# Perceiver block on one core: statistics before normalising, GpSimd normalises half of the tiles, first masks, keys and values between the query projections

## The chip, the cores and the metric

The kernel runs on one core of a Trainium2 chip, as one program. The metric is the device time of one execution in microseconds (us), median over several. Five engines work side by side and meet at semaphores: TensorE (PE; its weight loads are PEld), VectorE (DVE), ScalarE (ACT), GpSimd (POOL) and SyncE (SP), which here only issues DMAs. L12 is line 12 of the kernel before.

## The reference, cut to what matters

Three blocks follow each other on x (128 batches of 32 queries, width 128); each normalises its input. The change lies in front of, and at the start of, the first.

```python
x = x + xattn(layernorm(x), ctx_1024, ctx_1024, mask, Wq, bq, Wk, bk, Wv, bv, Wo, bo)
x = x + attn(layernorm(x), w_q, w_k, w_v, w_o)      # rotary, 16 query heads, 4 key heads
x = x + ffn(layernorm(x), Wg, W1, W2)               # 8 experts, one for each token
# xattn, 16 heads of width 8, 257 keys to a batch:
Q, K, V = heads(query @ Wq + bq), heads(key @ Wk + bk), heads(value @ Wv + bv)
energy = where(mask == 0, -1e9, Q K^T / sqrt(8)); out = softmax(energy) V; return out @ Wo + bo
```

## The kernel before

**Prologue.** The 4096 rows of x are 32 tiles of 128 rows (`X`), loaded in four quarters. For each quarter DVE takes statistics (`bn_stats`, L1424), works out mean and variance (L1388 to L1398), has ACT take the root (L603), inverts it (L1400) and normalises the quarter's eight tiles into `xn` (L1406), and only then goes on to the next. PE turns four tiles at a time (`turn_norm`, L488), ACT copies them (`xg`, L608), PE projects them with Wq (`queries`), ACT writes the queries (`QT`, L613). Eight such groups u = 0..7 make all queries. POOL waits for the last, then makes `SEL_Q` (L828), the first two tiles of queries by head (`QB`, L833) and four masked key rows (`MZ`, L840).

**Cross-attention.** It goes by pairs of batches p = 0..63. SP loads context (`CX`, eight DMAs, L516) and mask (`MK`, two DMAs, L522) of a pair; four pairs fit. DVE transposes the context (`turn_context`, `CT`, L1489), PE makes keys (`KS` after ACT, L630) and values (`VT`, L637), then scores (`energies`, tile name `energy`), turns probabilities and attends. In step p DVE transposes pair p + 3 and PE makes keys of p + 2, each behind and ahead of other work in a fixed order, so that a pair that comes late stops both engines.

**The last key.** Key 257 is handled apart. Its values `VL` are made by PE, copied by DVE (L1515) and stored by a DMA of ACT's queue into `v_last` (L667), behind ACT's first keys and values. SP waits for that store (`st_vl`), loads `VLT` from it in four DMAs (L539, 512 KB each), then issues a fill of 3483 KB (L543), and only behind these the context of pair 4. These lines of SP's program are the same before and after:

```python
sp.dma_start(ML[:, :], ..., allow_slow_non_contiguous=True).then_inc(ld_ml, 16)   # L535
sp.wait_ge(st_vl, 16)
for b in range(BT):
    sp.dma_start(VLT[b * SQ:(b + 1) * SQ, :, :], ...).then_inc(ld_vl, 16)         # L539
sp.dma_start(rows_in..., fill...).then_inc(filled, 16)                            # L543
with sp.Fori(1, NP // 4) as i:
    for k in range(4):
        load_pair(i * 4 + k, k, False)
```

**Small weights.** Ahead of `ML` SP issues 13 loads of small tables (semaphore `ld_s`, L528 to L532). DVE waits for all 13, makes `digits`, `sw_vg` and `wqk` from them (L1442 to L1454, 13 copies), which only the second and third block use, and then transposes the context of pair 0.

Of the kernel before, what the change touches and what calls it, by code (L numbers as in the profile page):

```python
# [13 lines left out]
ALU = mybir.AluOpType  # L14
# [58 lines left out]
def perceiver_block(nc, x, ctx_in, mask, Wq, bq, Wk, bk, Wv, bv, Wo, bo,  # L73
# [18 lines left out]
    with ExitStack() as ctx:  # L92
# [493 lines left out]
        def _(act):  # L586
# [12 lines left out]
            def root(u, h):  # L599
                if u % GX == 0:  # L600
                    act.wait_ge(n0_std, u // GX + 1)
                    part = std[:, u * 4:(u + GX) * 4]
                    nc.scalar.activation(part, part, ACT.Sqrt).then_inc(n0_rstd, 1)  # L603

            def evac_x(u, h):
                act.wait_ge(n0_tr, u + 1)
                wait_reuse(act, n0_q, u - 1)
                nc.scalar.activation(xg[:, h, :], psum[h][:, :], ACT.Copy).then_inc(n0_xt, 1)  # L608
# [7 lines left out]
            for u in range(NT // 4 + 1):  # L616
                if u < NT // 4:
                    root(u, u % 2)
                    evac_x(u, u % 2)
                if u == 1:  # L620
                    act.wait_ge(n0_bias, 1)
                if u:
                    evac_q(u - 1, (u - 1) % 2)
# [37 lines left out]
            nc.scalar.activation(warm[:, :], warm[:, :], ACT.Exp)  # L661
            evac_k(0, 0)
            evac_values(0, 0)
# [152 lines left out]
        def _(pool):  # L816
# [48 lines left out]
            tile(0, 0, True)  # L865
            tile(0, 1, True)
# [6 lines left out]
            tile(1, 1, False)  # L873
            pool.wait_ge(klt_ok, 1)
# [107 lines left out]
        def _(pe):  # L982
# [178 lines left out]
            pe.wait_ge(wqk_ok, 1)  # L1161
# [210 lines left out]
        def _(dve):  # L1372
# [9 lines left out]
            def moments_to_rstd(st_sem, rs_sem, count=1, tiles=slice(0, NT), done=None):  # L1382
# [16 lines left out]
                dve.wait_ge(rs_sem, count)  # L1399
# [420 lines left out]
```

## Time and profile before

| | |
|---|---|
| median of 3 runs | 813.57 us (811.36 to 815.04) |
| the profiled execution | 814.61 us, span 812.5 us |
| PE, DVE, ACT, POOL busy in the span | 86%, 78%, 63%, 47% |
| prologue, to the start of the first transposed context | 0 to 42.65 us |
| cross-attention | about 43 to 466 us |
| self-attention, router, experts | the rest |

An idle engine costs time only if what it waits for is what everything waits for. The chain of waits is followed from the last instruction back; where it runs over a queue that issues DMAs it is named after it (SPq, ACTq).

### The profile page before, as it was taken

The page shows a single profiled execution, that of the slowest core. Times are in us where ns is not written, and L with a number is a line of the kernel's source. Part 1 is how long each engine was busy: PE and PEld are TensorE (multiplying, and loading weights), DVE is VectorE, ACT ScalarE, POOL GpSimd, SP SyncE. Part 2 cuts the span into 40 slices and gives each one's busy share as a digit, 9 for nine tenths or more (in the row PEclk, how much of TensorE's full clock was granted, in tenths as well). Part 3 has the DMA queues.
Part 4 walks back from the last instruction along what each step waited for, and adds up shares of the span by engine and source line. Part 5 has one row for each costly group of instructions (what it writes and reads, how often), then busy time and mean ns, then how long its engine had stood idle before and what let it go on. Part 6 is the DMA issues. An engine that isn't in the chain of part 4 may idle for free.

```text
span 812.5 us, 27814 instructions
## 1 busy us (share of the span) xinstructions
PE 698.5 (86%) x9162; PEld 562.0 (69%) x9162; DVE 630.8 (78%) x1500; ACT 510.2 (63%) x1629; POOL 380.6 (47%) x380
## 2 busy tenths in 40 slices
PE   3572999999999999999999856799999689999565
PEld 1241767677777777777777645688888578889465
DVE  5462989899999999999999858589988656759721
ACT  1451777777777777787778624688888434545242
POOL 1250364456544654553544249477777320006365
PEclk9976999999999999999999979799999759999788
DMA  7558344444444444443440030000000000006980
GB/s 165 96 97 225 81 86 81 96 92 90 92 91 95 87 96 85 97 83 81 92 83 13 2 105 1 2 3 3 0 0 3 2 1 1 1 1 196 290 253 23
DMA packets 195179, 60.75 MB, mean 75 GB/s; under 512 B 147557, under 2 KB 193513, under 8 KB 195123
## 3 DMA queue, kind: packets, MB, share of 16 engines
q1 hardware_dynamic: 192000, 55.65, 30.7%
q0 software_dynamic: 1824, 3.96, 1.4%
q8 instruction: 35, 0.57, 0.3%
q10 hardware_dynamic: 1298, 0.40, 0.2%
q14 instruction: 22, 0.17, 0.1%
HBM read 51.58 MB, written 8.83 MB: 74 GB/s over the span
## 4 chain that ended last, share of the span: by engine, by line
PE 50%; SPq 17%; DVE 10%; issue 9%; ACT 7%; POOL 3%; ACTq 1%; DMA 1%; DVEq 0%; POOLq 0%
PE energy L485 22%; PE bank L485 15%; PE bank L488 13%; SPq L516 9%; ACT PR L644 6%; DVE STAT L1465 2%; SPq L522 2%; DVE X L1738 2%; SPq L566 1%; SPq L564 1%; POOL SX L907 1%; SPq L561 1%; POOL TQ L899 1%; ACTq L644 1%; SPq L539 1%
## 5 line engine op out<-in xcount | busy, mean ns | idle before, releaser
L644 ACT ACTIVATE PR<-energy,STAT 128x256 f32<-128x256 f32 x512 | 234.4, 482 | 107.5 <-DVE STAT L1465 107.5
L1465 DVE TENSOR_REDUCE STAT<-energy 128x512 f32 (+1 forms) x256 | 164.3, 685 | 27.2 <-PE energy L485 26.9
L488 PE MATMUL bank<-ident,PR 128*128 128x128 f32 x1024 | 152.5, 283 | 21.6 <-DVE PT L1482 16.8
L1482 DVE COPY PT<-bank 128x512 f32<-128x512 f32 x256 | 161.9, 672 | 1.3 <-PE bank L488 1.3
L488 PEld LDWEIGHTS bank<-ident,PR 128*128 128x128 f32 x1024 | 109.7, 142 | 52.6 <-issue 40.3
L833 POOL TENSOR_TENSOR QB<-QT,headmask 128x512 f32<-128x512 f32 x32 | 33.3, 1039 | 196.1 <-DMA MK<-in_mask_BxSxS_ik 122.1
L644 ACT ACTIVATION_READ_ACCUMULATOR PR<-energy,STAT (+1 forms) x512 | 110.1, 215 | 0.0
L840 POOL TENSOR_SCALAR MZ<-MK 128x512 bf16<-128x512 int32 x64 | 94.3, 1491 | 0.0
L485 PEld LDWEIGHTS bank<-wv_s,CT 128*128 128x128 f32 x512 | 68.7, 196 | 32.3 <-issue 31.8
L485 PE MATMUL bank<-CT,wk_s 128*128 128x512 f32 x128 | 68.5, 618 | 7.2 <-DVE CT L1489 7.2
L485 PE MATMUL bank<-PT,VT 128*32 128x128 f32 x2048 | 70.1, 278 | 0.2 <-DVE PT L1482 0.2
L485 PE MATMUL bank<-wv_s,CT 128*128 128x128 f32 x512 | 69.3, 280 | 0.3 <-DVE OC L1474 0.2
L485 PEld LDWEIGHTS bank<-PT,VT 128*32 128x32 f32 x2048 | 52.8, 110 | 21.3 <-DVE PT L1482 20.0
L485 PE MATMUL energy<-KS,QB 32*128 32x256 f32 x1024 | 66.1, 374 | 0.0
L1489 DVE STREAM_TRANSPOSE CT<-CX 128x512 f32<-128x512 f32 x64 | 44.9, 702 | 20.8 <-DMA CX<-in_ctx 16.9
L969 POOL DMA_INDIRECT rows_in<-PAY,SLOT x20 | 19.6, 978 | 83.4 <-DVE SLOT L1766 77.6
L630 ACT ACTIVATE KS<-bank,bias 128x512 f32<-128x512 f32 x64 | 46.2, 722 | 10.5 <-PE bank L485 10.5
L485 PEld LDWEIGHTS energy<-KS,QB 32*128 32x128 f32 x1024 | 49.4, 184 | 3.0
L485 PE MATMUL energy<-w_s,TQ 128*128 128x128 f32 x384 | 47.7, 277 | 0.0
L846 POOL TENSOR_TENSOR OC<-OC,headmask 128x512 f32<-128x512 f32 x32 | 33.3, 1039 | 30.5 <-DVE OC L1474 30.5
L485 PEld LDWEIGHTS energy<-w_s,TQ 128*128 128x128 f32 x384 | 46.2, 192 | 1.5
L637 ACT ACTIVATE VT<-bank 128x512 f32<-128x512 f32 x64 | 40.9, 639 | 1.0 <-PE bank L485 1.0
(268 smaller groups left out, 1340.6 us busy)
## 6 DMA issues: line engine op xcount, KB each, us to landing
CX<-in_ctx SPq DMA_DIRECT2D x512, 32.0 KB, 2.2
MK<-in_mask_BxSxS_ik SPq DMA_DIRECT2D x128, 128.0 KB
rows_in<-fill SPq DMA_DIRECT2D x1, 3483.0 KB, 19.0
X<-in_x SPq DMA_DIRECT2D x4, 512.0 KB, 7.7
VLT<-v_last SPq DMA_DIRECT2D x4, 512.0 KB, 8.2
QT<-in_L_ffn_W SPq DMA_DIRECT2D x16, 128.0 KB
OT<-in_L_ffn_W SPq DMA_DIRECT2D x16, 128.0 KB
PAY<-rows_in SPq DMA_DIRECT2D x2, 903.0 KB, 8.2
```

What stands on the lines that cost most here:

```text
L485: return nc.tensor.matmul(o, l, r, start=start, stop=stop, skip_group_check=True)
L488: return nc.tensor.transpose(o, i, ident[0:n, 0:n])
L516: sp.dma_start(CX[rows, k, e, :, :], ctx_in[bass.ds(2 * p + e, 1), 0:KEYS, rows] .rearrange("a (n j) i -> j (a n) i", j=32)).then_inc(ld_c ...
L630: nc.scalar.activation(KS[:, k % 2, :], psum[0][:, :], ACT.Identity, bias=bias[:, 1:2])\
L637: nc.scalar.activation(VT[:, k, :], psum[6], ACT.Copy).then_inc(ev_w, 1)
L644: nc.scalar.activation(PR[:, b, g, :], EB[:, g, e * KEYS:(e + 1) * KEYS], ACT.Exp, bias=STAT[:, bass.ds(t, 1), b, 1, g:g + 1].rearrange("p ...
L833: nc.gpsimd.tensor_tensor(QB[:, k, :, :, :], QT[:, bass.ds(t * P, P)].rearrange("p (b a q) -> p b a q", b=BT, a=1).broadcast_to([P, BT, 4, ...
L840: nc.gpsimd.tensor_scalar(MZ[:, k, :, :], MK[:, k, :, :], 0.0, None, ALU.is_equal).then_inc(pool_m, 1)
L846: nc.gpsimd.tensor_tensor(own, own, headmask[:, :].rearrange("p (a h c) -> p a h c", a=1, c=1).broadcast_to([P, BT, 4, SQ]), ALU.mult).the ...
L1465: V.tensor_reduce(STAT[:, bass.ds(t, 1), b:b + 2, 1, g:g + 1].rearrange("p a b g -> p (a b g)"), EB[:, g, :].rearrange("p (e k) -> p e k", ...
L1482: V.tensor_copy(PT[:, k % 2, e, 2 * half:2 * half + 2, :].rearrange("p g k -> p (g k)"), psum[1 if e else 7]).then_inc(ev_t, 1)
L1489: V.transpose(CT[:, k % 2, :], CX[:, k, :, :, :].rearrange("p e n i -> p (e n i)")).then_inc(ev_l, 1)
```

## The change

DVE takes the statistics of quarter q + 1 before it normalises quarter q. It normalises two tiles of each four, and POOL the other two, in `norm_queries` of its own. `digits`, `wqk` and `sw_vg` are made by POOL, behind the masks of pairs 4 to 7. SEL_Q and the first mask row stand on POOL between groups 3 and 4, the other three behind group 7. PE makes the last key's values and keys, and keys and values of pair 0, between groups 6 and 7, and DVE transposes pairs 0 and 1 around the last quarter. Copies of the turned tiles use banks 1 and 7 instead of 0 and 1, since bank 0 now takes keys. `moments_to_rstd` is split in `moments` and `inverse_root`. The core of the diff:

```diff
@@ -596,16 +598,15 @@
...
-            def root(u, h):
-                if u % GX == 0:
-                    act.wait_ge(n0_std, u // GX + 1)
-                    part = std[:, u * 4:(u + GX) * 4]
-                    nc.scalar.activation(part, part, ACT.Sqrt).then_inc(n0_rstd, 1)
+            def root(q):
+                act.wait_ge(n0_std, q + 1)
+                part = std[:, q * 4 * GX:(q + 1) * 4 * GX]
+                nc.scalar.activation(part, part, ACT.Sqrt).then_inc(n0_rstd, 1)
             def evac_x(u, h):
                 act.wait_ge(n0_tr, u + 1)
                 wait_reuse(act, n0_q, u - 1)
-                nc.scalar.activation(xg[:, h, :], psum[h][:, :], ACT.Copy).then_inc(n0_xt, 1)
+                nc.scalar.activation(xg[:, h, :], psum[7 if h else 1], ACT.Copy).then_inc(n0_xt, 1)
             def evac_q(u, h):
@@ -613,10 +614,15 @@
...
-            for u in range(NT // 4 + 1):
-                if u < NT // 4:
-                    root(u, u % 2)
-                    evac_x(u, u % 2)
+            root(0)
+            root(1)
+            for u in range(NT // 4 - 1):
+                if u == 2:
+                    root(2)
+                if u == 4:
+                    root(3)
+                    nc.scalar.activation(warm[:, :], warm[:, :], ACT.Exp)
+                evac_x(u, u % 2)
                 if u == 1:
                     act.wait_ge(n0_bias, 1)
                 if u:
@@ -658,8 +664,10 @@
...
-            nc.scalar.activation(warm[:, :], warm[:, :], ACT.Exp)
+            evac_x(NT // 4 - 1, 1)
+            evac_q(NT // 4 - 2, 0)
             evac_k(0, 0)
+            evac_q(NT // 4 - 1, 1)
             evac_values(0, 0)
             evac_k(0, 1)
@@ -822,10 +830,14 @@
...
-            pool.wait_ge(ld_wx, N_X)
-            pool.wait_ge(n0_qt, NT // 4)
-            nc.gpsimd.tensor_scalar(SEL_Q[:, :], query[:, :], BIG, None, ALU.mult).then_inc(sel_ok, 1)
+            def norm_queries(u, h):
+                if u % 2 == 0:
+                    pool.wait_ge(n0_inv, u // 2 + 1)
+                wait_reuse(pool, n0_tr, u - 1)
+                for j in (2, 3):
+                    t = u * 4 + j
+                    nc.gpsimd.tensor_scalar(xn[:, h, j, :], X[:, t, :], mv[:, t:t + 1, 0], rstd[:, t:t + 1],
+                                            ALU.subtract, ALU.mult).then_inc(n0_xp, 1)
...
@@ -862,8 +874,21 @@
...
-            tile(0, 0, True)
-            tile(0, 1, True)
+            for u in range(NT // 4):
+                norm_queries(u, u % 2)
+                if u == 3:
+                    pool.wait_ge(ld_wx, N_X)
+                    nc.gpsimd.tensor_scalar(SEL_Q[:, :], query[:, :], BIG, None, ALU.mult).then_inc(sel_ok, 1)
+                    pool.wait_ge(ld_mask[0], 32)
+                    masked_keys(0)
+            pool.wait_ge(n0_qt, 1)
+            queries_by_head(0, 0, True)
+            for k in (1, 2, 3):
+                pool.wait_ge(ld_mask[k], 32)
+                masked_keys(k)
+                if k == 1:
+                    queries_by_head(1, 1, True)
+            pool.wait_ge(n0_qt, NT // 4)
             pool.wait_ge(brow_sp, 1)
             nc.gpsimd.tensor_tensor(X[:, :, :], X[:, :, :],
@@ -871,6 +896,21 @@
...
             tile(1, 0, False)
             tile(1, 1, False)
+            pool.wait_ge(ld_s, N_S)
+            pool.wait_ge(zero_ok, 2)
+            nc.gpsimd.tensor_copy(digits[:, :, :].rearrange("p r k -> p (r k)"), digit_s).then_inc(wqk_ok, 1)
+            qv = sw_q[:, :].rearrange("p (h a f) -> p h a f", h=NG * 4, a=2)
+            kv = sw_k[:, :].rearrange("p (k g a f) -> p k g a f", k=NG, g=1, a=2)
+            for a in range(2):
+                for w, s in ((0, a), (1, 1 - a)):
+                    nc.gpsimd.tensor_copy(wqk[:, w, :].rearrange("p (h a f) -> p h a f", h=NG * 4, a=2)[:, :, a, :],
+                                          qv[:, :, s, :]).then_inc(wqk_ok, 1)
+                    nc.gpsimd.tensor_copy(
+                        wqk[:, 2 + w, :].rearrange("p (k g a f) -> p k g a f", k=NG, g=4, a=2)[:, :, :, a, :],
+                        kv[:, :, :, s, :].broadcast_to([P, NG, 4, 4])).then_inc(wqk_ok, 1)
+            for g in range(NG):
+                nc.gpsimd.tensor_copy(sw_vg[:, g, g * HD:(g + 1) * HD], sw_v[:, g * HD:(g + 1) * HD]).then_inc(wqk_ok, 1)
             pool.wait_ge(klt_ok, 1)
...
@@ -995,17 +1035,14 @@
             def turn_norm(u, h):
                 wait_reuse(pe, n0_xt, u - 1)
                 for j in range(4):
-                    pe.wait_ge(n0_xn, 4 * u + (j + 1))
-                    last = tr(psum[h][:, j * P:(j + 1) * P], xn[:, h, j, :])
+                    pe.wait_ge(n0_xp if j >= 2 else n0_xn, 2 * u + (j % 2 + 1))
+                    last = tr(psum[7 if h else 1][:, j * P:(j + 1) * P], xn[:, h, j, :])
                 last.then_inc(n0_tr, 1)
             def queries(u, h):
                 pe.wait_ge(n0_xt, u + 1)
...
@@ -1098,16 +1135,23 @@
...
+            for u in range(NT // 4 + 1):
+                if u < NT // 4:
+                    turn_norm(u, u % 2)
+                if u:
+                    queries(u - 1, (u - 1) % 2)
+                if u == NT // 4 - 2:
+                    pe.wait_ge(dve_clt, 1)
+                    pe.wait_ge(ld_wx, N_X)
+                    pe.wait_ge(brow_sp, 1)
+                    mm(psum[4][:, 0:P], CLT, wv_s[:, :]).then_inc(pe_vl, 1)
+                    mm(psum[5][:, 0:P], wk_s[:, :], CLT).then_inc(pe_kl, 1)
+                    keys(0, 0)
+                if u == NT // 4 - 1:
+                    values(0, 0)
+            keys(0, 1)
             pe.wait_ge(n0_qt, NT // 4)
-            pe.wait_ge(brow_sp, 1)
             pe.wait_ge(sel_ok, 1)
-            pe.wait_ge(ld_wx, N_X)
-            pe.wait_ge(dve_clt, 1)
-            mm(psum[4][:, 0:P], CLT, wv_s[:, :]).then_inc(pe_vl, 1)
-            mm(psum[5][:, 0:P], wk_s[:, :], CLT).then_inc(pe_kl, 1)
-            keys(0, 0)
-            values(0, 0)
-            keys(0, 1)
             pe.wait_ge(vl_ok, 1)
             pe.wait_ge(klt_ok, 1)
...
@@ -1413,48 +1459,49 @@
...
-                for j in range(4):
+                for j in (0, 1):
...
-            for q in range(NLX):
+            def quarter_moments(q):
                 dve.wait_ge(ld_x[q], 16)
-                with dve.Fori(q * TX // 4, (q + 1) * TX // 4) as i:
-                    for j in range(4):
...
+                for t in range(q * TX, (q + 1) * TX):
...
-                moments_to_rstd(n0_std, n0_rstd, q + 1, slice(q * TX, (q + 1) * TX))
-                if q == 1:
-                    dve.wait_ge(brow_all, 1)
-                    V.tensor_copy(BROW[:, :], psum[5][:, 0:P]).then_inc(brow_sp, 1)
-                    dve.wait_ge(pe_clt, 1)
-                    V.tensor_copy(CLT, psum[6][:, 0:P]).then_inc(dve_clt, 1)
-                if q == 0:
-                    dve.wait_ge(ld_q, N_Q)
-                    V.tensor_scalar(qbias[:, :], bias[:, 0:1], -SCALE, None, ALU.mult).then_inc(n0_bias, 1)
-                    dve.wait_ge(brow_pe, 1)
-                    V.tensor_tensor(brow[:, :], brow[:, :], psum[4][0:1, 0:P], ALU.add).then_inc(brow_ok, 1)
+                moments(n0_std, slice(q * TX, (q + 1) * TX))
+            def quarter_norm(q):
+                part = slice(q * TX, (q + 1) * TX)
+                dve.wait_ge(n0_rstd, q + 1)
+                V.reciprocal(rstd[:, part], std[:, part]).then_inc(n0_inv, 1)
+                dve.wait_ge(n0_inv, q + 1)
                 for u in range(q * TX // 4, (q + 1) * TX // 4):
                     norm_queries(u, u % 2)
-            dve.wait_ge(ld_s, N_S)
-            link(V.tensor_copy(digits[:, :, :].rearrange("p r k -> p (r k)"), digit_s))
-            dve.wait_ge(zero_ok, 2)
-            for g in range(NG):
-                V.tensor_copy(sw_vg[:, g, g * HD:(g + 1) * HD], sw_v[:, g * HD:(g + 1) * HD])
-            qv = sw_q[:, :].rearrange("p (h a f) -> p h a f", h=NG * 4, a=2)
-            kv = sw_k[:, :].rearrange("p (k g a f) -> p k g a f", k=NG, g=1, a=2)
-            for a in range(2):
-                for w, s in ((0, a), (1, 1 - a)):
-                    V.tensor_copy(wqk[:, w, :].rearrange("p (h a f) -> p h a f", h=NG * 4, a=2)[:, :, a, :],
-                                  qv[:, :, s, :])
-                    last = V.tensor_copy(
-                        wqk[:, 2 + w, :].rearrange("p (k g a f) -> p k g a f", k=NG, g=4, a=2)[:, :, :, a, :],
-                        kv[:, :, :, s, :].broadcast_to([P, NG, 4, 4]))
-            last.then_inc(wqk_ok, 1)
+            def turn_context(i, r):
...
+                dve.wait_ge(ld_ctx[k], 128 * (i + r // 4) + 128)
+                wait_reuse(dve, pe_v, p - 1)
+                V.transpose(CT[:, k % 2, :], CX[:, k, :, :, :].rearrange("p e n i -> p (e n i)")).then_inc(ev_l, 1)
+            quarter_moments(0)
+            quarter_moments(1)
+            quarter_norm(0)
+            dve.wait_ge(ld_q, N_Q)
+            V.tensor_scalar(qbias[:, :], bias[:, 0:1], -SCALE, None, ALU.mult).then_inc(n0_bias, 1)
+            dve.wait_ge(brow_pe, 1)
+            V.tensor_tensor(brow[:, :], brow[:, :], psum[4][0:1, 0:P], ALU.add).then_inc(brow_ok, 1)
+            quarter_moments(2)
+            quarter_norm(1)
+            dve.wait_ge(pe_clt, 1)
+            V.tensor_copy(CLT, psum[6][:, 0:P]).then_inc(dve_clt, 1)
+            dve.wait_ge(brow_all, 1)
+            V.tensor_copy(BROW[:, :], psum[5][:, 0:P]).then_inc(brow_sp, 1)
+            quarter_moments(3)
+            quarter_norm(2)
+            turn_context(0, 0)
+            quarter_norm(3)
+            turn_context(0, 1)
...
@@ -1510,12 +1551,10 @@
...
-            turn_context(0, 0)
             dve.wait_ge(pe_vl, 1)
             V.tensor_copy(VL[:, :], psum[4][:, 0:P]).then_inc(vl_ok, 1)
             dve.wait_ge(pe_kl, 1)
             V.tensor_scalar(KLT[:, :], psum[5][:, 0:P], bias[:, 1:2], None, ALU.add).then_inc(klt_ok, 1)
-            turn_context(0, 1)
             turn_context(0, 2)
             step_range(dve, step)
             step(NP // 4, 0)
```

How the order on three engines changes. On DVE, from the normalising of the last quarter to the third context, before (`xn` are normalised tiles, `CT` a transposed context, `VL` the last key's values; two of the eight COPY rows of `wqk` shown):

```order
L1406 TENSOR_SCALAR xn<-X,mv,rstd 128x128 x8
L1442 CAST digits<-sort_c 128x45
L1447 COPY sw_vg<-sw_v 128x8 x4
L1452 COPY wqk<-sw_q 128x16x4
L1454 COPY wqk<-sw_k 128x16x4
...
L1489 STREAM_TRANSPOSE CT<-CX 128x512
L1515 COPY VL<-energy 128x128
L1517 TENSOR_SCALAR KLT<-energy,bias 128x128
L1489 STREAM_TRANSPOSE CT<-CX 128x512 x2
```

The same stretch after the change, from the normalising of the third quarter on:

```order
L1452 TENSOR_SCALAR xn<-X,mv,rstd 128x128 x4
L1485 STREAM_TRANSPOSE CT<-CX 128x512
L1476 RECIPROCAL rstd<-std 128x8
L1452 TENSOR_SCALAR xn<-X,mv,rstd 128x128 x4
L1485 STREAM_TRANSPOSE CT<-CX 128x512
L1555 COPY VL<-energy 128x128
L1557 TENSOR_SCALAR KLT<-energy,bias 128x128
L1485 STREAM_TRANSPOSE CT<-CX 128x512
L1512 TENSOR_REDUCE STAT<-energy 128x2 x4
```

The 13 small copies, and the wait for the small tables ahead of them, are gone from DVE's path to the first contexts.

On POOL, from the addition of the output bias to the loop of cross-attention, after the change (`OC`, `OT` gather a tile's output, `KLB` and `MLB` belong to the last key):

```order
L894 TENSOR_TENSOR X<-X,BROW 128x4096
...
L864 TENSOR_TENSOR OT<-OC 128x128
L902 CAST digits<-sort_c 128x45
L907 COPY wqk<-sw_q 128x16x4
L909 COPY wqk<-sw_k 128x16x4
...
L913 COPY sw_vg<-sw_v 128x8 x4
L915 TENSOR_TENSOR KLB<-KLT,head 128x2048
L920 TENSOR_SCALAR MLB<-ML 128x32
...
L845 TENSOR_TENSOR QB<-QT,headmask 128x512
```

Before, `KLB` stood directly behind `OT`; the 13 copies now stand between them, ahead of the masks of pairs 8 and 9.

On ACT the order up to the store of the last key's values, after the change:

```order
L609 ACTIVATE xg<-bank 128x512
L614 ACTIVATE QT<-energy,qbias 128x512
L636 ACTIVATE KS<-bank,bias 128x512
L614 ACTIVATE QT<-energy,qbias 128x512
L643 ACTIVATE VT<-bank 128x512
L636 ACTIVATE KS<-bank,bias 128x512
L675 DMA v_last<-VL 128x128
```

Before, both QT rows stood ahead of the first KS; the first keys have moved in between, and v_last stands behind the same two KS and one VT as before.

## Rows read from the trace of the kernel before

**Rows 1.** Busy time of each engine by stretch (us, with instructions)
```profile
core 0: us, PE busy (x) PEld busy (x) DVE busy (x) ACT busy (x) POOL busy (x), PEclk, DMA share, GB/s
39.00:50.00 11.00, 6.60 (x32) 3.68 (x32) 4.95 (x18) 1.97 (x3) 11.00 (x5) 0.55 0.23 8
50.00:76.00 26.00, 10.68 (x120) 7.79 (x116) 7.96 (x13) 9.63 (x36) 2.37 (x1) 0.81 0.97 230
```

**Rows 2.** The chain that ended last, 30 to 150 us: start us, us, what
```profile
37.94 2.16 DMA sw_o<-in_L_attn_w_o
...
43.40 5.50 PE bank L485 x12
48.94 1.57 DMA v_last<-VL
50.52 0.34 SPq L539
...
58.76 9.02 SPq L516
...
143.41 2.25 DMA CX<-in_ctx
```

**Rows 3.** Timeline 38 to 62 us, SP's queue: start us, us, engine line what
```profile
38.61 0.45 SPq L535 DMA_DIRECT2D ML<-in_mask_BxSxS_ik  x1
...
50.52 5.40 SPq L539 DMA_DIRECT2D VLT<-v_last  x4
...
55.96 2.38 SPq L543 DMA_DIRECT2D rows_in<-fill  x1
```

**Rows 4.** Timeline of DVE, 60 to 92 us; idle before the row in brackets
```profile
76.53 0.71 DVE L1489 STREAM_TRANSPOSE CT<-CX 128x512 f32<-128x512 f32 x1 [16.74 <-DMA CX<-in_ctx]
```

**Rows 5.** Busy time by single microseconds, columns as in the first group
```profile
40.00:41.00 1.00, 0.00 (x0) 0.00 (x0) 0.84 (x4) 0.00 (x0) 1.00 (x2) 0.50 1.32 9
41.00:42.00 1.00, 0.00 (x0) 0.00 (x0) 1.00 (x10) 0.00 (x0) 1.00 (x1) 0.50 0.82 6
42.00:43.00 1.00, 0.00 (x0) 0.00 (x0) 1.00 (x5) 0.00 (x0) 1.00 (x2) 0.50 0.00 0
```

**Rows 6.** Timeline of the prologue, 0 to 40 us
```profile
6.28 1.04 DVE L1424 BATCH_NORM_STATS2 stats<-X  x4 [5.43 <-DMA X<-in_x]
...
13.83 1.63 DVE L1424 BATCH_NORM_STATS2 stats<-X  x8
...
16.22 0.17 DVE L1398 SCALAR_TENSOR_TENSOR std<-mv,std 128x8 f32<-128x8 f32 x1
...
18.22 2.13 DVE L1406 TENSOR_SCALAR xn<-X,mv,rstd 128x128 f32<-128x128 f32 x8
...
29.12 2.14 DVE L1406 TENSOR_SCALAR xn<-X,mv,rstd 128x128 f32<-128x128 f32 x8
...
33.92 0.69 ACT L613 ACTIVATE QT<-energy,qbias 128x512 f32<-128x512 f32 x1 [0.40 <-PE energy L485]
```

**Rows 7.** Groups of DVE instructions, 11 to 32 us: busy us, mean ns | idle before, releaser
```profile
L1400 DVE RECIPROCAL rstd<-std 128x8 f32<-128x8 f32 x4 | 0.8, 202 | 3.9 <-ACT std L603 3.9
L1431 DVE COPY BROW<-energy 128x128 f32<-128x128 f32 x1 | 0.3, 291 | 0.0
```

**Rows 8.** Groups of POOL instructions, 34 to 135 us, same columns
```profile
L840 POOL TENSOR_SCALAR MZ<-MK 128x512 bf16<-128x512 int32 x12 | 17.9, 1509 | 0.0
...
L828 POOL TENSOR_SCALAR SEL_Q<-query 128x128 bf16<-128x128 f32 x1 | 0.6, 552 | 31.5 <-ACT QT L613 31.5
```

**Rows 9.** Timeline 649 to 657 us (router)
```profile
653.06 2.32 POOL L960 COPY PAY<-X 128x2560 f32<-128x2560 f32 x1
...
655.34 0.21 POOL L962 CAST PAY<-sort_c 128x20 int32<-128x20 f32 x1
```

**Rows 10.** Instructions on tile X: ns min/median/max, first and last start us
```profile
L1406 DVE TENSOR_SCALAR PAY<-X,mv,rstd x20: 333/338/2342, 649.9 to 661.4; 128x128 f32<-128x128 f32 x20
```

**Rows 11.** Timeline 108 to 124 us (pairs 8 and 9)
```profile
109.40 0.33 POOL L880 TENSOR_SCALAR MLB<-ML 128x32 f32<-128x32 int32 x1
...
112.40 1.04 POOL L833 TENSOR_TENSOR QB<-QT,headmask 128x512 f32<-128x512 f32 x1 [2.67 <-DMA MK<-in_mask_BxSxS_ik]
...
115.38 0.39 PE L485 MATMUL energy<-MZ,SEL_Q 32*128 32x512 bf16 x4
```

More of the change, by code:

```diff
@@ L297, in perceiver_block @@
         n0_rstd = sem("n0_rstd")
+        n0_inv = sem("n0_inv")
         n0_xn = sem("n0_xn")
+        n0_xp = sem("n0_xp")
         n0_tr = sem("n0_tr")
@@ L1005, in queries @@
                 mm(psum[2 + h][:, :], wq_s[:, :], xg[:, h, :]).then_inc(n0_q, 1)
-            pipeline(pe, [(0, turn_norm), (1, queries)], NT // 4, 2, 2)
             def keys(i, r):
@@ L1158, in _ @@
                     out_project(u - 1, (u - 1) % 2)
-            pe.wait_ge(wqk_ok, 1)
+            pe.wait_ge(wqk_ok, 9 + NG)
             pe.wait_ge(ld_s, N_S)
@@ L1380, in link, with moments @@
                 dve.wait_ge(dve_c, chain[0])
-            def moments_to_rstd(st_sem, rs_sem, count=1, tiles=slice(0, NT), done=None):
+            def moments(st_sem, tiles=slice(0, NT)):
                 me, mo = stats[:, tiles, 1], stats[:, tiles, 4]
@@ L1398, in moments_to_rstd, with inverse_root @@
                 V.scalar_tensor_tensor(std[:, tiles], mv[:, tiles, 1], 0.25, std[:, tiles], ALU.mult, ALU.add).then_inc(st_sem, 1)
-                dve.wait_ge(rs_sem, count)
+            def inverse_root(rs_sem, done=None, tiles=slice(0, NT)):
+                dve.wait_ge(rs_sem, 1)
                 link(V.reciprocal(rstd[:, tiles], std[:, tiles]))
@@ new lines, in quarter_moments @@
+                for t in range(q * TX, (q + 1) * TX):
+                    V.bn_stats(stats[:, t, :], X[:, t, :]).then_inc(dve_st1, 1)
+                dve.wait_ge(dve_st1, (q + 1) * TX)
+                moments(n0_std, slice(q * TX, (q + 1) * TX))
[4 more added lines that the diff above has]
+                dve.wait_ge(n0_inv, q + 1)
@@ L1450, in _ @@
-            for a in range(2):
-                for w, s in ((0, a), (1, 1 - a)):
-                    V.tensor_copy(wqk[:, w, :].rearrange("p (h a f) -> p h a f", h=NG * 4, a=2)[:, :, a, :],
-                                  qv[:, :, s, :])
-                    last = V.tensor_copy(
-                        wqk[:, 2 + w, :].rearrange("p (k g a f) -> p k g a f", k=NG, g=4, a=2)[:, :, :, a, :],
-                        kv[:, :, :, s, :].broadcast_to([P, NG, 4, 4]))
-            last.then_inc(wqk_ok, 1)
+            def turn_context(i, r):
+                p, k, t = pair(i, r)
+                dve.wait_ge(ld_ctx[k], 128 * (i + r // 4) + 128)
+                wait_reuse(dve, pe_v, p - 1)
+                V.transpose(CT[:, k % 2, :], CX[:, k, :, :, :].rearrange("p e n i -> p (e n i)")).then_inc(ev_l, 1)
@@ L1483, in evac_turned @@
                               psum[1 if e else 7]).then_inc(ev_t, 1)
-            def turn_context(i, r):
-                p, k, t = pair(i, r)
-                dve.wait_ge(ld_ctx[k], 128 * (i + r // 4) + 128)
-                wait_reuse(dve, pe_v, p - 1)
-                V.transpose(CT[:, k % 2, :], CX[:, k, :, :, :].rearrange("p e n i -> p (e n i)")).then_inc(ev_l, 1)
             def step(i, r):
@@ L1585, in _ @@
             dve.wait_ge(dve_st1, 2 * NT)
-            moments_to_rstd(n1_std, n1_rstd, done=n1_shift)
+            moments(n1_std)
+            inverse_root(n1_rstd, n1_shift)
             def rotary(t, j):
@@ L1630, in _ @@
             dve.wait_ge(a_st, NT)
-            moments_to_rstd(n2_std, n2_rstd)
+            moments(n2_std)
+            inverse_root(n2_rstd)
             def norm_router(u, h):
@@ L1665, in _ @@
             nb = len(places)
+            dve.wait_ge(wqk_ok, 9 + NG)
             for r, place in enumerate(places):
```

3 lines of the change are left out of this document (removed).

## The prediction

> **What bounds the kernel now.** I read the busy time by stretch first, since the change lies in the first 50 us and its effect must be read there. Between 39 and 50 us PE is busy for 6.60 of 11 us at a granted clock of 0.55, and the DMA engines are nearly idle (0.23). Between 50 and 76 us it is the other way round: PE is busy for 10.68 of 26 us and the DMA engines for 0.97 of it [rows 1]. So one hole in the kernel's start is a hole of DMA work, and right behind it stands a hole of compute.
>
> The chain of waits ties them together [rows 2]. It runs over SP's queue to 37.94 us, where the last of the small tables is issued. That load lands at 40.1, DVE makes its 13 copies from the tables and transposes pair 0, PE makes the first keys and values (43.40, 5.50 us), ACT issues the store of the last key's values (48.94, 1.57 us), and only then, at 50.52, SP goes on with `VLT`. From there the chain stays on SP and its DMAs up to 143.41. The first context DMA of pair 4 alone holds the queue for 9.02 us from 58.76, behind the 2 MB of `VLT` and the 3.5 MB of the fill.
>
> What SP itself had to do is seen in its timeline: `ML` is issued at 38.61 for 0.45 us, then nothing until 50.52 [rows 3]. SP is free at 39.06 and waits 11.46 us for `st_vl`. What that queue brings is what everybody waits for: DVE sits idle for 16.74 us until pair 4's context lands and is transposed at 76.53 [rows 4], and behind that transpose, in DVE's fixed order, stand the probabilities that PE needs. That PE could be faster in the first four pairs is worth nothing: it would only wait longer for pair 4.
>
> **The change part by part.** The store `v_last` is what the time hangs on, so the question is when it lands and what SP then still waits for.
>
> *Small tables.* DVE no longer waits for them ahead of pair 0, and the 13 copies leave it. The chain's piece from 37.94 over 40.1 to the transpose goes.
>
> *The prologue on DVE.* Eight statistics and the seven steps to the variance took from 13.83 to 16.39, 2.56 us a quarter [rows 6], four of them 10.2. Eight normalisations take 2.13 us, so 16 take 4.3. Four reciprocals are 0.8 (202 ns each), and the 3.9 us that DVE waited for ACT's root are covered now by the next quarter's statistics [rows 7]. Four small operations at about 0.29 (as BROW's) are 1.2, and two transposes of 0.71 [rows 4] are 1.4. From the landing of the first quarter at 6.28 that is 17.9, so DVE is through at about 24.2, where before the last normalisation ended at 31.26.
>
> *POOL's half.* No row has a POOL normalisation. The nearest is SEL_Q, one 128x128 operation with one factor, 0.55 us [rows 8]; a copy runs 2560 elements in 2.32 us and 20 in 0.21 [rows 9], which for 128 gives 0.3. I take 0.55, the same operation and size, as the upper end and the one nearest. Four to a quarter are 2.2 us against DVE's 1.1, so the last quarter ends 1.1 us later on POOL: 25.3. The first mask row, 1.5 us between groups 3 and 4 [rows 8], falls in the time in which DVE takes statistics; if the mask is late it pushes groups 4 and 5 by a microsecond or two, within the margin below.
>
> *From the last normalised tile to the store.* Before, 31.26 to the end of the last QT at 34.61 took 3.35 us [rows 6]. Then come pair 0's values and pair 1's keys; the whole piece of keys, values and keys was 5.5 us in the chain, at the lower clock [rows 2], and is an upper bound since part of it now lies between the projections. So the store is issued by about 25.3 + 3.35 + 5.5 = 34.2 and lands 1.57 later, at 35.7.
>
> SP is free at 39.06, and nothing in the change touches its order. So `st_vl` has been reached 3.4 us before SP asks, and `VLT` starts at 39.06: **-11.46 us**. The prologue gains more than that on DVE's side, and the rest buys nothing.
>
> *What the earlier start runs into.* `ML` is 4096 single words, and its transfer filled the DMA engines for 1.32 and 0.82 of the two microseconds from 40 to 42, with 9 and 6 GB/s, and nothing after 42 [rows 5]. Before, it was through long ahead of `VLT`; now `VLT` stands right behind it in the same queue. The cost lies between nothing, if `VLT`'s own issuing (5.40 us for four [rows 3]) leaves that much room, and the full 2.14. I take half: **+1.1**.
>
> *The 13 copies on POOL.* They stand between pairs 7 and 8. There POOL finished `MLB` at 109.73 and sat idle for 2.67 us until the mask of pair 9 came [rows 11], and PE's scores of pair 8 followed at 115.38 with no gap to speak of, so what goes beyond 2.67 is paid. By the copy's two rows (0.21 us for 20 elements, 0.9 ns more for each) eight of 64 elements, one of 45 and four of 8 are 3.0 us; at the price of `MLB`, 0.33 each, they are 4.3. The lower bound is nothing: all inside the idle time. I take the copy's own rows: **+0.4**, at most 1.6.
>
> *The rest costs nothing.* ACT's table load ahead of the exponents (moved between the queries), the banks, the unrolled loops, the addition of the bias to X on POOL lie beside the idle stretch before pair 4. That is their cover, and it gets longer: what stands ahead of it comes some 14.7 us earlier (store issued at 34.2 instead of 48.94), pair 4 only 10, so DVE's 16.7 us become some 21.
>
> **The sum** is -11.46 + 1.1 + 0.4 = -10.0. The profiled execution had 814.61 us around its span of 812.5, and ran 1.04 above the median of 813.57. Against itself it gives 804.6, against the median 803.6.
>
> **The rivals.**
>
> *A. DVE and POOL stand in each other's way.* This one speaks against the split. While POOL copied 2560 elements for 2.32 us, one of DVE's normalisations took 2342 ns instead of 338 [rows 9, 10]: it was held to the end of POOL's instruction. In the prologue both now normalise at the same time. If every one of DVE's 16 is held for a whole one of POOL's, that adds 16 x 0.55 = 8.8 us: the store lands at 44.5, 5.4 us after SP is free, and the `ML` term falls away. The time is then 803.6 + 5.4 - 1.1 = 807.9. Against it: most of DVE's work in the prologue is not normalising, and POOL is idle for half of a quarter. The Trainium skill says this as a rule (SBUF — State Buffer, Who interferes with whom): the second port pair is locked by one of the two for a whole instruction. By that rule, and these rows agree, the two halves cannot overlap at all. The rival decides only if it costs more than the 3.4 us of margin. Chance 0.10.
>
> *B. The gain is partly given back before 146 us.* After pair 4 the chain is on SP, but PE, DVE and POOL run nearly as late: the chain leaves SP at 143.41 and PE is then the bound. If the pairs from 4 on run closer to PE than the chain shows, POOL's delay and the colder start add up to half of the gain: 808 to 811. For it speaks that PE's scores of pair 8 follow POOL's mask at once [rows 11]. Chance 0.08.
>
> *C. The gain does not appear,* since pair 4 is bound by something that does not move with `VLT`. Against it is that the DMA engines are nearly idle up to 50 us and busy for 0.97 of the 26 us behind it [rows 1], and what fills them starts at 50.52. 813.6, chance 0.03.
>
> *D. More than the sum,* if SP's later queue also runs smoother, 799 or less. Nothing in the rows speaks for it. Chance 0.04.
>
> *E. Slower.* The 13 copies on POOL have strided and repeated operands, and no row has such copies on POOL. From (10.4 + 2.67) / 13 = 1.0 us for one they eat the whole gain, since pair 8's masks wait behind them, and pair 8's scores for those. At 1.5 us each the kernel is at 803.2 + 19.5 - 2.67 = 820.0. Against it: `QB` has strided and repeated operands too and takes 1.04 us for 512 elements [rows 11], 2 ns each, so patterns alone do not make 64 elements cost a microsecond. Chance 0.05.
>
> The forecast has what is left, 0.70.
>
> **How the numbers follow.** The bounds of the terms give 803.6 - 1.5 = 802.1 (both costs nothing) and 813.57 - 11.46 + 2.14 + 1.6 = 805.9. The three runs of before lie up to 2.2 us from their median, so the forecast's own range is 800 to 807.5. Rival A at 807.9 and the better part of B are taken in by an upper end of 808.5, D's near part by a lower end of 799.5; C, E and the far parts are left out, some 0.15 to 0.2. A measurement of this kernel can tell about 0.5%, 4.1 us, from no change. Faster by more than that are the forecast, A, D and a part of B: 0.87. Within it C and the rest of B: 0.08. Slower E: 0.05.
>
> **What would show each step.** In the trace of after: `VLT` is issued directly behind `ML`, near 39.1, with no wait of SP (if SP waits, the store is late, as in A); `v_last` is issued before 37; DVE's 16 normalisations have a mean near 338 ns, or near 800 if held; pair 4's context is transposed at 65 to 67 instead of 76.5, and the idle time ahead of it is nearer 20 us; POOL's 13 copies take about 3 us and the scores of pair 8 stand at 104 to 106. The prediction is wrong if SP's queue to `ML` itself takes longer than before, if the 26 us from `VLT` to the transpose of pair 4 do not move as a block, or if the distance from that transpose to the end of cross-attention grows.

## The result, and the profile after

The changed kernel takes 805.22 us in the median of 4 runs (802.70 to 807.57), the kernel before 813.59 beside it: a ratio of 0.9912, 95% interval 0.9894 to 0.9929, or 8.4 us less. The profiled execution had 805.83 us around a span of 803.8, 8.7 below the span of before.

The place is the one that was forecast. Timeline of SP's queue in the changed kernel, 36 to 80 us (start us, us, what):

```profile
39.60 0.45 SPq L537 DMA_DIRECT2D ML<-in_mask_BxSxS_ik  x1
40.09 7.70 SPq L541 DMA_DIRECT2D VLT<-v_last  x4
47.83 2.15 SPq L545 DMA_DIRECT2D rows_in<-fill  x1
50.40 16.40 SPq L518 DMA_DIRECT2D CX<-in_ctx  x8
```

SP goes from `ML` to `VLT` without a wait, where it waited 11.5 us before [rows 3]. The store that it used to wait for is early; timeline of the changed kernel, 28 to 48 us:

```profile
33.28 0.71 DVE L1485 STREAM_TRANSPOSE CT<-CX 128x512 f32<-128x512 f32 x1 [2.77 <-PE bank L487]
...
34.82 0.40 PE L487 MATMUL energy<-MZ,SEL_Q 32*128 32x512 bf16 x4
...
34.93 0.37 ACTq L675 DMA_DIRECT2D v_last<-VL  x1
```

It is issued 14.0 us earlier (34.93 against 48.94 [rows 2]), and the first scores of PE stand at 34.82 instead of 48.83. But pair 4 comes only 7.7 us earlier. Timeline of DVE in the changed kernel, 36 to 84 us; the bracket is the idle time before the row:

```profile
44.51 1.28 DVE L1529 COPY PT<-bank 128x512 f32<-128x512 f32 x2
68.84 0.71 DVE L1485 STREAM_TRANSPOSE CT<-CX 128x512 f32<-128x512 f32 x1 [23.05 <-DMA CX<-in_ctx]
```

This row answers to [rows 4]: 68.84 for 76.53, and the idle time has grown from 16.74 to 23.05 us. So 6.3 of the 14.0 us that the prologue gained are waited away here. The same in the busy time by stretch, columns as in [rows 1]:

```profile
39.00:50.00 11.00, 8.06 (x103) 5.88 (x102) 5.11 (x9) 7.52 (x28) 8.82 (x1) 1.00 0.88 130
50.00:76.00 26.00, 5.73 (x23) 4.73 (x24) 6.07 (x11) 4.65 (x18) 0.00 (x0) 0.54 0.86 199
```

The DMA engines' share between 39 and 50 us has risen from 0.23 to 0.88: the hole of DMA work is filled, and the hole of PE's work is now in the second stretch (5.73 of 26 us busy, 10.68 before).

From the transpose of pair 4 to the end nothing of note moved. The exponents of the last key (ACT, `DIFF`) stood at 476.65 before and stand at 467.87 now, 400.1 and 399.0 us behind that transpose.

### The profile page after: what moved, and what is told of

Its sections match the earlier page's. It is cut to its first block, busy times and chain, and to the rows that moved or that the text cites. A ratio compares the mean times of both kernels' runs of the same rounds, so it can differ in the third digit from the quotient of the medians.

```text
span 803.8 us, 27728 instructions
## 1 busy us (share of the span) xinstructions
PE 697.8 (87%) x9162; PEld 563.4 (70%) x9162; DVE 623.8 (78%) x1471; ACT 510.0 (63%) x1629; POOL 395.5 (49%) x409
## 4 chain that ended last, share of the span: by engine, by line
PE 49%; SPq 16%; DVE 10%; issue 9%; ACT 7%; POOL 4%; ACTq 1%; DMA 1%; DVEq 0%; POOLq 0%
PE energy L487 22%; PE bank L487 15%; PE bank L490 13%; SPq L518 8%; ACT PR L650 6%; DVE X L1778 3%; DVE STAT L1512 2%; SPq L524 2%; POOL SX L947 1%; SPq L541 1%; SPq L566 1%; POOL TQ L939 1%; SPq L577 1%; SPq L568 1%; ACTq L650 1%
## 5 line engine op out<-in xcount | busy, mean ns | idle before, releaser
L1512 DVE TENSOR_REDUCE STAT<-energy 128x512 f32 (+1 forms) x256 | 164.2, 684 | 26.4 <-PE energy L487 26.4
L487 PE MATMUL bank<-CT,wk_s 128*128 128x512 f32 x128 | 66.5, 602 | 0.0
L487 PE MATMUL energy<-w_s,TQ 128*128 128x128 f32 x384 | 47.7, 277 | 0.0
L983 POOL TENSOR_TENSOR SX<-SX,sinv 128x512 f32<-128x512 f32 x32 | 33.5, 1048 | 16.2 <-DVE sinv L1656 16.2
```

The source lines that it names most:

```text
L487: return nc.tensor.matmul(o, l, r, start=start, stop=stop, skip_group_check=True)
L983: nc.gpsimd.tensor_tensor(SX[:, j, :, :], SX[:, j, :, :], sinv[:, j, :].rearrange("p (n a) -> p n a", a=1).broadcast_to([P, 16, SQ]), ALU. ...
L1512: V.tensor_reduce(STAT[:, bass.ds(t, 1), b:b + 2, 1, g:g + 1].rearrange("p a b g -> p (a b g)"), EB[:, g, :].rearrange("p (e k) -> p e k", ...
```

## The experiments

All are compared with the kernel before on the same chip, whose median there was 812.0 to 813.6 us; the ratios compare best across the rows. A profile of each gave the two places that the theory speaks of: the start of `VLT`, and the transpose of pair 4 on DVE.

| kernel | median us | ratio (95%) | VLT starts | pair 4 transposed | between |
|---|---|---|---|---|---|
| before | 813.6 | 1 | 50.52 | 76.53 | 26.0 |
| changed | 805.2 | 0.9912 (0.9894 to 0.9929) | 40.09 | 68.84 | 28.8 |
| e1, copies only | 806.4 | 0.9924 (0.9903 to 0.9946) | 43.15 | 69.81 | 26.7 |
| e2, copies back | 815.9 | 1.0043 (1.0028 to 1.0059) | 52.52 | 78.79 | 26.3 |
| e3, DVE normalises all | 804.6 | 0.9899 (0.9872 to 0.9927) | 39.26 | 67.72 | 28.5 |
| e4, ML late | 801.8 | 0.9876 (0.9849 to 0.9902) | 38.69 | 65.05 | 26.4 |
| e10, copies back, bias late | 810.0 | 0.9977 (0.9955 to 0.9999) | 46.93 | 73.95 | 27.0 |
| e5, VLT and fill late | 785.1 | 0.9678 (0.9650 to 0.9706) | late | 47.48 | |
| e6, before, VLT and fill late | 791.3 | 0.9752 (0.9716 to 0.9788) | late | 58.32 | |
| e9, all late | 780.2 | 0.9602 (0.9564 to 0.9641) | late | 43.72 | |
| e11, before, copies off, all late | 787.4 | 0.9698 (0.9675 to 0.9721) | late | 52.66 | |
| e12, e9, DVE normalises all | 780.4 | 0.9617 (0.9591 to 0.9643) | late | 43.88 | |

**One part alone (e1).** The 13 copies leave DVE; all else is the kernel before.

```diff
-            dve.wait_ge(ld_s, N_S)
-            link(V.tensor_copy(digits...)); ...            # 13 copies on DVE
             turn_context(0, 0)
...
             tile(1, 1, False)
+            pool.wait_ge(ld_s, N_S); ...                   # the same 13 copies on GpSimd
```

> The kernel before, with one part of the change alone: digits, wqk and sw_vg are made by GpSimd behind the masks of pair 7, as in the changed kernel; the prologue is that of before. Theory (only the moment counts at which SP may go on with VLT): pair 0 is transposed right behind the last normalisation at 31.3, the last key's values are stored at about 40.5, VLT starts at about 42 with ML already through, and pair 4 is transposed 26 us later at 68. That is where the changed kernel has it (68.84), so the time is 804 to 806.5 us. Rival (the gain comes from statistics ahead of normalising and from GpSimd's half): 811 to 814 us.

The time came out as the theory has it. The timeline of e1, 28 to 62 us:

```profile
31.50 0.70 DVE L1486 STREAM_TRANSPOSE CT<-CX 128x512 f32<-128x512 f32 x1
...
39.42 0.36 ACTq L667 DMA_DIRECT2D v_last<-VL  x1
...
43.15 6.03 SPq L539 DMA_DIRECT2D VLT<-v_last  x4
```

Pair 0 is transposed at 31.50 instead of 42.65, and that alone brings 0.76% against 0.88% for the whole change; the intervals overlap. Statistics ahead, GpSimd's half and the interleaving add nothing that these runs can tell.

The places differ from the changed kernel's all the same. The store in e1 was issued at 39.42 and took 3.7 us to land, where it took 1.57 before [rows 2]; the chain that ended last of e1 has it:

```profile
39.42 3.71 DMA v_last<-VL
```

So SP still waited for it in e1, and `VLT` started 3.1 us later than in the changed kernel (43.15 against 40.09). Of these 3.1 us the changed kernel keeps 1.0 at pair 4 (68.84 against 69.81), since its `VLT` stands right behind `ML`.

**That part undone (e2), and what was found there (e10).** In e2 DVE makes the copies again, between the last normalisation and pair 1, and GpSimd no longer makes them.

```diff
             quarter_norm(3)
+            dve.wait_ge(ld_s, N_S)
+            link(V.tensor_copy(digits...)); ...            # 13 copies on DVE
             turn_context(0, 1)
```

> The changed kernel, with digits, wqk and sw_vg made by DVE again, behind the last normalisation and ahead of the transpose of pair 1. Theory: DVE waits for the small tables until 41 and makes its copies until about 43.7, the store of the last key's values is issued at about 46, VLT starts near 47.7 and pair 4 is transposed near 73.7: 809.5 to 812 us, most of the gain lost although the prologue is as fast as in the changed kernel up to there. Rival (a faster prologue is what pays): stays at 804 to 806.5 us.

The direction was right and the size was not: 815.9 us, slower than the kernel before, with `VLT` at 52.5 instead of the expected 47.7. Its timeline, 36 to 52 us, has the reason:

```profile
38.07 8.80 POOL L894 TENSOR_TENSOR X<-X,BROW 128x4096 f32<-128x4096 f32 x1
...
40.57 6.34 DVE L1491 CAST digits<-sort_c 128x45 int32<-128x45 f32 x1 [14.29 <-DMA sw_o<-in_L_attn_w_o]
...
46.95 0.39 DVE L1496 COPY sw_vg<-sw_v 128x8 f32<-128x8 f32 x4
```

DVE's copy of 45 elements starts at 40.57 and ends with GpSimd's addition, at 46.9. e10 takes that addition out of the way by one more wait in front of it:

```diff
             pool.wait_ge(n0_qt, NT // 4)
+            pool.wait_ge(ld_mask[0], 64)                   # the mask of pair 4
             pool.wait_ge(brow_sp, 1)
             nc.gpsimd.tensor_tensor(X[:, :, :], X[:, :, :], BROW...)
             tile(1, 0, False)
```

> e2_copies_back once more (DVE makes the 13 copies ahead of pair 1), with GpSimd's addition of the bias to X (8.8 us) moved behind the mask of pair 4, out of the time of these copies. In e2_copies_back the first copy took 6.34 us, to the very end of that addition, instead of 0.30. Theory (that GpSimd instruction held DVE's copy): the copy is back at 0.3 us, the store of the last key's values is issued 6 us earlier, near 45, pair 4 is transposed near 73, and the time is 808.5 to 811.5 us, where e2_copies_back had 815.9. Rival (the copy is slow for another reason, such as its source just landed): about 815 us again.

Timeline of DVE in e10, 36 to 60 us:

```profile
41.15 0.19 DVE L1492 CAST digits<-sort_c 128x45 int32<-128x45 f32 x1 [14.74 <-DMA sw_o<-in_L_attn_w_o]
41.37 0.39 DVE L1497 COPY sw_vg<-sw_v 128x8 f32<-128x8 f32 x4
```

The copy takes 0.19 us, the store is issued at 45.36 instead of 50.94, and the time is 810.0. So GpSimd's addition held the copy, and with that out of the way the copies on DVE cost what was expected of them: most of the gain.

**GpSimd's half undone (e3).**

```diff
-                for j in (0, 1):
+                for j in range(4):          # DVE's norm_queries; GpSimd's call removed
```

> The changed kernel, but DVE normalises all four tiles of a group and GpSimd none. Theory: the store of the last key's values still lands before SP is through with ML at 40.0, so VLT starts where it does and the time is 804 to 806.5 us. Rival (GpSimd's half matters): the prologue grows by more than the cover and the time is 807 us or more.

804.6 us: no loss. The store is issued at 34.78 (34.93 with the split) although DVE has twice the normalisations.

**ML out of VLT's way (e4).**

```diff
-            sp.dma_start(ML[:, :], mask...)                # ahead of VLT
...
             with sp.Fori(1, NP // 4) as i: ...
+            sp.dma_start(ML[:, :], mask...)
```

> The changed kernel, with ML (4096 single words) loaded behind SP's loop over the pairs, and MLB made behind GpSimd's loop. Theory (ML's transfer right ahead of VLT in the same queue costs the 2.7 us by which VLT to pair 4 has grown, and its issue 0.5): VLT starts at 39.6, is issued in about 5.4 us instead of 7.7, and pair 4 is transposed 26 us behind its start, at 65.6: 801.5 to 803 us. Rival (the 2.7 us come from something else, such as a fuller DMA queue with the first three pairs' loads): pair 4 at 68, 804.5 to 805.5 us.

Timeline of SP's queue in e4, 30 to 50 us:

```profile
38.69 5.94 SPq L539 DMA_DIRECT2D VLT<-v_last  x4
44.67 2.19 SPq L543 DMA_DIRECT2D rows_in<-fill  x1
```

`VLT` is issued in 5.94 us instead of 7.70, and pair 4 follows 26.4 us behind its start instead of 28.8. The median is 3.4 us below the changed kernel's, but the intervals of the two ratios overlap, so the time alone does not settle it. The distances do: 26.0 to 27.0 us stand in every kernel in which `ML` is through before `VLT` starts or comes later (before, e1, e2, e10, e4), and 28.5 and more only where it stands right ahead (changed, e3).

**VLT and fill behind the loop, in both kernels (e5, e6).** If these two hide the prologue, the change must be worth more once they are gone.

```diff
-            sp.wait_ge(st_vl, 16); sp.dma_start(VLT...)    # 4 loads
-            sp.wait_ge(fill_ok, 2); sp.dma_start(rows_in, fill)
             with sp.Fori(1, NP // 4) as i: ...
+            sp.wait_ge(st_vl, 16); sp.dma_start(VLT...)
             sp.wait_ge(ev_o, NP)
             sp.dma_start(w1_s...); sp.dma_start(w2_s...)
+            sp.wait_ge(fill_ok, 2); sp.dma_start(rows_in, fill)
```

> The changed kernel, but SP issues the four loads of VLT behind its loop over the pairs and the fill behind the load of the expert weights; both are needed only after cross-attention. Theory (all that the prologue could gain is hidden behind VLT and the fill, which stand ahead of pair 4): pair 4 is transposed at about 47 instead of 68.84, the 23 us of idle DVE shrink to a few, and the rest keeps its 399 us: 782 to 786 us. Rival (pair 4 is late for a reason of its own, or what follows cannot keep up): 795 us or more.

> The kernel before with the same two moves as e5_vlt_fill_late (VLT behind the loop, fill behind the expert weights), otherwise untouched. Theory: now the prologue is on the path itself. Its first scores stand at 48.8 against 34.8 of the changed kernel, pair 4 is there before it is wanted, and the kernel is at 792 to 796 us: the change is then worth 9 to 13 us over this one. Rival (the prologue of the change brings nothing even where it is not hidden): within 3 us of e5_vlt_fill_late.

Both are far faster, 785.1 and 791.3 us, 20 to 22 us below the kernels that they start from. The difference between them was 6.2 us (8.2 between the profiled executions) and not the expected 9 to 13. So the change is worth no more without `VLT` and the fill in front of pair 4 than with them: these 5.5 MB delay both kernels alike, and do not hide the prologue. The first scores are 13.3 us apart (34.11 and 47.44), those of pair 8 9.2 (86.42 and 95.65). Timeline of DVE in e5, 26 to 95 us:

```profile
47.48 0.71 DVE L1486 STREAM_TRANSPOSE CT<-CX 128x512 f32<-128x512 f32 x1 [2.41 <-DMA CX<-in_ctx]
...
66.06 0.71 DVE L1486 STREAM_TRANSPOSE CT<-CX 128x512 f32<-128x512 f32 x1 [0.63 <-DMA CX<-in_ctx]
...
73.20 0.71 DVE L1486 STREAM_TRANSPOSE CT<-CX 128x512 f32<-128x512 f32 x1 [1.34 <-DMA CX<-in_ctx]
```

In e5 DVE still waits for contexts, 4.4 us in these three rows, since the 13 tables and `ML` keep SP busy until 39.4; e6 has no such wait in the same stretch. Its transpose of pair 4, in the timeline of DVE in e6, 40 to 95 us:

```profile
58.32 0.70 DVE L1490 STREAM_TRANSPOSE CT<-CX 128x512 f32<-128x512 f32 x1
```

**Everything behind the loop (e9, e11, e12).** The tables and `ML` go too. e9 starts from the changed kernel, e11 from e1, e12 is e9 with all normalisations on DVE.

```diff
-            for dst, src in small_s: ...                   # 13 loads, and ML, ahead of the loop
             with sp.Fori(1, NP // 4) as i: ...
             sp.wait_ge(st_vl, 16); sp.dma_start(VLT...)
+            sp.dma_start(ML...)
+            for dst, src in small_s: ...
```

> The changed kernel with VLT, ML, the small tables and (behind the expert weights) the fill all behind SP's loop; MLB and the 13 copies move on GpSimd accordingly, the copies to just ahead of the expert weights' remainder. Theory: pair 4 is loaded by about 39, before DVE wants it at 44, so no load holds up the start; against e5_vlt_fill_late it gains the 3 to 4 us that pair 4 is still late there: 778 to 783 us. Rival (from 47 us on the pace is set by PE or by SP's 6.3 us a pair anyway): the same as e5_vlt_fill_late within 1.5 us.

> e1_copies_only (the prologue of before, the 13 copies off DVE) with the loads moved as in e9_all_late: VLT, ML and small tables behind SP's loop, the fill behind the expert weights, MLB and the copies likewise. Beside e9_all_late it shows what the other half of the change (statistics ahead, GpSimd's half, first masks, keys and values between the projections) is worth where nothing hides it. Theory: its first scores stand near 39, as in e1_copies_only, against 32.8 in e9_all_late, pair 4 is there in time in both, so it is 5 to 7.5 us slower than e9_all_late: 785 to 788 us. Rival (that half is worth nothing, or the pace of the pairs absorbs it): within 2 us of e9_all_late, 779 to 782 us.

> e9_all_late, but DVE normalises all four tiles of a group and GpSimd none. GpSimd's normalisations took 0.79 us each in the changed kernel and DVE's 0.34, and where DVE did all the first scores stood within 0.3 us of the changed kernel's. Theory (GpSimd's half saves DVE 4 us and costs as much, since a group waits for GpSimd's slower two): within 1.5 us of e9_all_late, 779 to 782 us. Rival (the split pays where the prologue is not hidden): 783 us or more.

Timeline of PE in e9, and then in e11, 30 to 50 us:

```profile
32.84 0.40 PE L487 MATMUL energy<-MZ,SEL_Q 32*128 32x512 bf16 x4
...
38.80 0.40 PE L487 MATMUL energy<-MZ,SEL_Q 32*128 32x512 bf16 x4 [1.25 <-ACT PR L651]
```

```profile
41.78 0.39 PE L485 MATMUL energy<-MZ,SEL_Q 32*128 32x512 bf16 x4
...
47.74 0.40 PE L485 MATMUL energy<-MZ,SEL_Q 32*128 32x512 bf16 x4 [1.25 <-ACT PR L645]
```

The first scores are 8.9 us apart, the kernels 7.2 (780.2 and 787.4; e12, on the chip of e11, is 7.0 below it). A part of the 8.9 belongs to the one execution: that of e11 ran 2.1 us above its median, with a granted clock of 0.50 from 32 to 34 us, where e1 with the same prologue had 1.00. So with nothing in front of pair 4 the second half of the change, within the noise in e1's comparison, is worth 7 us. GpSimd's part in that is none: e12 has the first scores at 32.99 and 780.4 us. Whether the 7 us come from the statistics ahead or from the first masks, keys and values between the projections was not run. e9 is the best version, 4.0% below the kernel before, and e12 is as fast with less in it.

## Why the prediction was right

The forecast was 803.6 us, in a range of 799.5 to 808.5, and 805.2 was measured. Its steps in their order:

*The store decides, and only until SP is free.* Shown by e1 and e3: stores at 39.4, 34.8 and 34.9 gave 806.4, 804.6 and 805.2 us. And by e2 and e10: later stores (50.9, 45.4) move pair 4 with them.

*The store is issued by 34.2 and lands by 35.7.* It was issued at 34.93, but the sum that led there was right by luck. A normalisation on GpSimd took 0.79 us and not 0.55. Instructions on tile `xn` in the changed kernel (ns min/median/max, first and last start us):

```profile
L1452 DVE TENSOR_SCALAR xn<-X,mv,rstd x16: 332/346/476, 11.3 to 27.5; 128x128 f32<-128x128 f32 x16
L839 POOL TENSOR_SCALAR xn<-X,mv,rstd x16: 782/792/891, 11.4 to 28.2; 128x128 f32<-128x128 f32 x16
```

The first mask came late as well: GpSimd waited 1.75 us for it at 21.07, and the groups behind it too. DVE idled 5.1 us for the turned tiles, so the last normalisation ended on GpSimd near 29.0 and not at 25.3. From there to the store it took 5.9 us and not 3.35 + 5.5, since most of the keys and values lie between the projections. TensorE's clock had a part that the sum does not have: it was granted 0.59 and 0.56 from 24 to 26 and 26 to 28 us, the lower of its two levels (1.2 GHz) for most of that time, after PE had been busy for 0.33 of the 2 us before. In e4, with the same prologue and a clock of 1.00 there, the store was issued at 33.04.

The landing was mis-sized. The store took 3.8 us and not 1.57, so it had landed at 38.7, and the margin before SP was free (40.05) was 1.3 us and not 3.4. DMA issues of the changed kernel, 30 to 70 us (KB, us from issue to landing):

```profile
v_last<-VL ACTq DMA_DIRECT2D x1, 64.0 KB, 3.8
```

*VLT starts at 39.06.* It started at 40.09. SP's own queue was a microsecond later. In the profiles of all these kernels it reaches the issue of `ML` between 38.2 and 39.6 us, also where nothing ahead of it differs (38.2 in e1, 38.6 before), so this is scatter of one execution and no effect of the change.

*ML costs 1.1 us, at most 2.14.* This is the term of the sum that was mis-sized. Against the kernel before it is 2.7 us (28.8 - 26.0), against e4 2.4. The distances themselves scatter by a microsecond: the mean of the two kernels with `ML` right ahead is 28.6, of the five without it 26.5, so 2.1 us, which is the upper bound and twice what was put in. `VLT`'s issuing left no room for the transfer: its four issues took 7.70 and 7.20 us with `ML` right ahead, 5.40 to 6.03 without, and the fill moved back with them.

*The 13 copies on GpSimd cost 0.4 us.* They cost nothing. Timeline of GpSimd in the changed kernel, 36 to 112 us:

```profile
96.83 0.22 POOL L902 CAST digits<-sort_c 128x45 int32<-128x45 f32 x1
...
98.92 3.68 POOL L915 TENSOR_TENSOR KLB<-KLT,head 128x2048 f32<-128x2048 f32 x1
102.68 0.33 POOL L920 TENSOR_SCALAR MLB<-ML 128x32 f32<-128x32 int32 x1
103.62 1.04 POOL L845 TENSOR_TENSOR QB<-QT,headmask 128x512 f32<-128x512 f32 x1 [0.62 <-DMA MK<-in_mask_BxSxS_ik]
```

All 13 took 2.1 us, since each starts before the one ahead has ended, and of the 2.67 us of idle time 0.62 are left. The scores of pair 8 stand at 106.71, 37.9 us behind the transpose of pair 4; before it was 38.9.

*The sum* was -11.46 + 1.1 + 0.4 = -10.0. Measured in the profiles it is -10.4 + 2.7 - 1.1 = -8.8 up to the last exponents. The -1.1 is the 1.1 us by which the 400 behind pair 4 are shorter. Nearly all of it stands between the scores of pairs 6 and 7, 7.16 us apart before and 6.05 after. In the other kernels the distance from pair 4 to these exponents is 395 to 399; no run aimed at it, and its cause stays open. That the sum came within 1.6 us of the median is in part luck: the term of `ML` was too small, and this piece made up for most of it.

*The rivals.* A (DVE held by GpSimd) did not happen in the changed kernel: DVE's normalisations have a median of 346 ns beside GpSimd's, against 340 before. The same hold did happen in e2, with another pair of instructions. The Trainium skill (SBUF — State Buffer, Who interferes with whom) gives the lock as held for a whole instruction by whichever of the two issues first, against DVE instructions in a mode that uses both port pairs (copies, casts and tensor_scalar can be in one), whatever GpSimd's instruction is. e2 and e10 agree with it; the normalisations do not, as four of DVE's ended in 1.17 us while the first two of GpSimd's were running. B, C and E are refuted by the distance behind pair 4, by the row of pair 4 and by the 2.1 us of the copies. D did not occur. e5 and e9 show that there was more to have in the queue ahead of pair 4, 20 and 25 us, but by moving loads that the change leaves where they are.

## What to carry to other kernels

When a stretch is shortened, look for the next queue that everyone waits for and at what is parked in it. Here the prologue became 14 us shorter, of which 8.4 arrived: SP was still issuing the first contexts, the 13 tables and `ML` until 40.05, so `VLT` started only 10.4 us earlier, and `ML` right ahead of it took some 2 us back. The 5.5 MB of `VLT` and fill, which nobody needed for another 400 us, stood ahead of the first context that was wanted; they cost both kernels some 20 us, and with them gone the change was worth no more (6.2 us). With the tables and `ML` moved as well it was 25 us, three times as much as the whole change.

A wait that one engine makes for data used much later (13 copies of small tables) can hold up all that stands behind it, so test that part alone before crediting the rest.

## What the runs showed of the hardware

- A long GpSimd instruction with two tensor inputs (128x4096, 8.8 us) held a DVE copy of 128x45 for 6.34 us, which takes 0.19 without it (e2, e10). GpSimd normalisations of 128x128 (one tensor input and two scalars of a partition) did not hold DVE's: four in 1.17 us. Timeline of the changed kernel, 5 to 22 us:

```profile
11.34 1.17 DVE L1452 TENSOR_SCALAR xn<-X,mv,rstd 128x128 f32<-128x128 f32 x4
11.41 3.31 POOL L839 TENSOR_SCALAR xn<-X,mv,rstd 128x128 f32<-128x128 f32 x4 [8.15 <-DVE rstd L1476]
```

- DVE's instruction was not what decided there. The same DVE normalisation, 0.34 us alone, took 2.34 us beside a GpSimd copy of 128x2560 [rows 9, 10], and in e3 up to 1.05 us where GpSimd made `QB`. Timeline of GpSimd in e3, 18 to 31 us, and then the instructions on `xn` in e3, 25 to 29 us:

```profile
27.05 1.07 POOL L845 TENSOR_TENSOR QB<-QT,headmask 128x512 f32<-128x512 f32 x1
```

```profile
L1451 DVE TENSOR_SCALAR xn<-X,mv,rstd x9: 333/340/1051, 24.7 to 28.6; 128x128 f32<-128x128 f32 x9
```

So the difference lies with GpSimd's instruction. It is not the number of its tensor inputs alone, since the copy has one as the normalisation has; which property decides was not tried.

- The same normalisation takes 0.34 us on DVE and 0.79 on GpSimd, where a plain copy of 128x64 takes 0.24.
- A load of 4096 single words right in front of 512 KB loads on the same queue made what follows them 1.4 to 2.7 us later, by which two profiles one compares, 2.1 between the means.
- A store of 64 KB landed 1.6 us after its issue where the DMA engines' share was 0.15 (before, e2, e10), and after 3.1 to 4.4 us where other loads were under way (share 0.24 in e11, 0.64 to 0.78 in the changed kernel, e1, e3, e4, e5, e9 and e12). The share is not the whole account: in e6 it was 0.42 and the store landed after 1.6 us.
